# Dealing the work at the ends of the two attention halves: statistics over heads, a tile table moved back, a causal mask by TensorE for two batches

## The reference

```python
x = x + _L0_attn_a_ref(_layernorm(x), wq, bq, wk, bk, wv, bv, wo, bo)    # causal, 16 heads of 8
x = x + _L0_ffn_ref(_layernorm(x), Wr, Wg, Wu, Wd)
x = x + _L0_attn_b_ref(_layernorm(x), W_qkv, b_qkv, W_proj, b_proj)      # not causal, softmax of a
x = x + _L0_ffn_ref(_layernorm(x), Wr, Wg, Wu, Wd)                       # scaled negative distance
```

## Time and profile before

| | us |
|---|---|
| median of 3 timed runs | 1205.51 |
| lowest and highest of them | 1203.42, 1205.73 |
| the profiled execution, its own time | 1201.22 |
| its span, first to last instruction | 1198.8 |
| busy: TensorE | 1031.9 (86%) |
| busy: VectorE | 763.5 (64%) |
| busy: ScalarE | 672.4 (56%) |
| busy: GpSimd | 538.9 (45%) |

### The profile page before, as it was taken

One profiled execution on the slowest core, in us unless ns is written; L12 is line 12 of the kernel. 1 busy time (PEld: TensorE's weight loads), 2 busy tenths in 40 slices (PEclk: granted clock), 3 DMA queues, 4 the chain that ended last, 5 costly groups with the idle time before them and its releaser, 6 DMA issues.

```text
span 1198.8 us, 28758 instructions
## 1 busy us (share of the span) xinstructions
PE 1031.9 (86%) x9198; PEld 719.2 (60%) x9198; DVE 763.5 (64%) x2364; ACT 672.4 (56%) x1399; POOL 538.9 (45%) x1010
## 2 busy tenths in 40 slices
PE   3998999896789989999798879998977689899990
PEld 1444555452358889999444434443443489899990
DVE  5687777968548333366778888888767573234442
ACT  2465767553524445555377769887836445455550
POOL 2243444333850630344688645655626416103555
PEclk9999999996858999999778889998967799999995
DMA  6355444662125877887644324333121258778974
GB/s 158 92 133 142 100 103 98 179 140 61 40 70 154 267 230 235 258 270 221 143 110 100 97 56 108 82 92 84 44 56 58 91 171 282 217 227 263 280 218 111
DMA packets 201722, 175.02 MB, mean 146 GB/s; under 512 B 19812, under 2 KB 160616, under 8 KB 201576
## 3 DMA queue, kind: packets, MB, share of 16 engines
q1 hardware_dynamic: 193384, 156.41, 47.4%
q0 software_dynamic: 8192, 16.79, 4.7%
HBM read 122.99 MB, written 50.14 MB: 144 GB/s over the span
## 4 chain that ended last, share of the span: by engine, by line
PE 44%; DVE 15%; POOL 9%; issue 6%; DMA 4%; SPq 1%; ACT 1%; POOLq 0%; ACTq 0%; DVEq 0%
PE psS L1358 9%; PE psT L1365 9%; PE psO L316 4%; PE psN L1381 4%; PE psO L1381 4%; PE psS L350 3%; POOL xn L1259 3%; DVE mx L662 3%; POOL prow L736 2%; PE psO L959 2%; PE psN L323 1%; PE psT L358 1%; PE psM L1346 1%; DMA eo<-ysb 1%; POOL part L749 1%
## 5 line engine op out<-in xcount | busy, mean ns | idle before, releaser
L662 DVE TENSOR_REDUCE mx<-psS 128x3 f32<-128x384 f32 (+1 forms) x512 | 311.1, 617 | 117.9 <-PE psS L377 62.4
L350 PE MATMUL psS<-kst,qst 48*128 48x256 bf16 (+1 forms) x1024 | 200.9, 284 | 57.2 <-DVE mx L662 42.6
L549 ACT ACTIVATE pT<-psT,scb 128x512 f32<-128x512 f32 x256 | 194.0, 778 | 56.7 <-PE psT L358 55.3
L1421 DVE TENSOR_TENSOR hT<-sg,psT 128x512 f32<-128x512 f32 x142 | 97.5, 686 | 160.3 <-PE psT L1365 126.1
L358 PE MATMUL psT<-qst,kst 50*128 50x256 bf16 (+1 forms) x1024 | 194.0, 279 | 5.4 <-DMA qst<-scr_m 2.4
L1245 POOL DMA_INDIRECT xg<-xn,slot x128 | 123.5, 965 | 149.9 <-DVE ysb L1416 86.5
L780 POOL TENSOR_SCALAR_AFFINE_SELECT pT<-pT 128x256 f32<-128x256 f32 x256 | 104.0, 414 | 134.0 <-ACT pT L544 132.2
L350 PEld LDWEIGHTS psS<-kst,qst 48*128 48x128 bf16 x1024 | 65.7, 97 | 156.8 <-DVE mx L662 82.7
L1358 PE MATMUL psS<-xTt,wgc 128*128 128x128 f32 x1136 | 153.5, 279 | 5.0 <-issue 5.0
L544 ACT ACTIVATE pT<-psT 128x384 f32<-128x384 f32 x256 | 122.6, 491 | 57.7 <-PE psT L358 56.2
L1365 PE MATMUL psT<-xTt,wuc 128*128 128x128 f32 x1136 | 151.8, 277 | 0.4 <-DMA wuc<-in_L_ffn_Wu 0.3
(11 more groups left out here) (227 smaller groups left out, 1605.2 us busy)
## 6 DMA issues: line engine op xcount, KB each, us to landing
wgc<-in_L_ffn_Wg SPq DMA_DIRECT2D x142, 256.0 KB
wuc<-in_L_ffn_Wu SPq DMA_DIRECT2D x142, 256.0 KB
scr_part<-part SPq DMA_DIRECT2D x128, 128.0 KB, 2.1
qst<-scr_part SPq DMA_DIRECT2D x64, 192.0 KB, 3.7
kst<-scr_part SPq DMA_DIRECT2D x64, 192.0 KB, 4.5
xin<-xg SPq DMA_DIRECT2D x142, 64.0 KB
eo<-ysb SPq DMA_DIRECT2D x142, 64.0 KB
scr_part<-part SPq DMA_DIRECT2D x32, 192.0 KB, 1.9
```

Source lines behind the costliest of these rows:

```text
L350: return nc.tensor.matmul(ps[:, c0:c0 + n], q_[r64, t, q0], k_[r64, t, 0:n], start=(half == 0), stop=True, skip_group_check=True)
L549: nc.scalar.activation(pT[:, g % 8, 0:cols], psT[g % 2][:, 0:cols], ACT.Exp, scale=scb[r][:, 0, i:i + 1], bias=scb[r][:, 1, i:i + 1]).then ...
L662: nc.vector.tensor_reduce(mx3[:, u, 0:n, pos:pos + 1].rearrange("p a b -> p (a b)"), psS[h % 2][:, 0:kcols(L)].rearrange("p (a k) -> p a k ...
L1421: nc.vector.tensor_tensor(out=hT[(n0 + k) % FETCH][:].rearrange("p a c -> p (a c)"), in0=sg[p][:], in1=psT[p][:], op=ALU.mult).then_inc(f[ ...
```

## The change

- Steps 17 and 18 of layer 0 (T of the batches 14 and 15, `MASKED = B - 2`): the select on GpSimd and its semaphore go; TensorE adds the mask to T by a matmul of the identity with a second triangle `tritb` over the two diagonal squares; `pv_quad` waits for the exponential. GpSimd makes `tritb` at the start (two operations more).
- Step 18, both layers: the statistics of group 1's 12 blocks are dealt over heads 0 to 8 by `dve_ln_at`, its tokens over heads 10 to 13, three a head.
- Group 0's stage 8 (tile table) goes from step 16, head 5 (layer 0) and step 17, head 2 (layer 1) to step 18, head 15; so does stage 2 (weights) from step 15, head 15 and step 16, head 12.
- Layer 1: the 16 tokens of GpSimd stand as 8 behind the split of step 14 and 8 behind that of step 15.
- Both layers: the load of Silu's activation table stands behind the first two tile copies of the feed-forward part, no more before them.

```diff
@@ pv_quad
-                after(pe, s["pT"], 16 * b + 4 * q + 4)
+                if L.causal and b >= MASKED:
+                    after(pe, s["exp"], 16 * b + 4 * q + 4)
+                else:
+                    after(pe, s["pT"], 16 * b + 4 * q + 4)
@@ pe_step, behind scores_t(1)
+                    if L.causal and bT >= MASKED:
+                        diag = psT[1 - par][:, 0:3 * P].rearrange("p (a k) -> p a k", a=3)[:, 0:3:2, :]
+                        last_t = nc.tensor.matmul(diag, identb[:], tritb[:].unsqueeze(1).to_broadcast([P, 2, P]),
+                                                  start=False, stop=True, skip_group_check=True)
                     last_t.then_inc(s["ST"], 1)
@@ pool_step
                     after(pool, s["exp"], 16 * bT + h + 1)
-                    d = pT[:, (h ^ 1) % 8, 0:384].rearrange("p (a k) -> p a k", a=3)[:, 0:3:2, :]
...
+                    if bT < MASKED:
+                        d = pT[:, (h ^ 1) % 8, 0:384].rearrange("p (a k) -> p a k", a=3)[:, 0:3:2, :]
...
@@ act_tile
             if k == 0:
                 tokens(0)
                 tokens(1)
+                nc.scalar.activation(junk[0:1, 0, 0:1], ones_row[0:1, 0:1], ACT.Silu)
@@ pool_beside
-                if l == 1 and j == 15 and h == 1:
+                if l == 1 and j in (14, 15) and h == H:
                     pool.wait_ge(s_ln[2], 1)
-                    for k in range(SIZE[0]):
+                    for k in range((j - 14) * SIZE[0] // 2, (j - 13) * SIZE[0] // 2):
@@ act_beside
-                if j == 19 and h == 15:
-                    nc.scalar.activation(junk[0:1, 0, 0:1], ones_row[0:1, 0:1], ACT.Silu)
@@ dve_beside
                         dve_counts(dve, 0)
-                        dve_route_part(dve, 0, 2)
-                if l == 0 and j == 16 and h < 6:
+                if l == 0 and j == 16 and h < 5:
                     dve_route_part(dve, 0, h + 3)
...
-                if l == 1 and j == 16 and h == 12:
-                    dve_route_part(dve, n, 2)
...
-                if l == 1 and j == 17 and h < 3:
+                if l == 1 and j == 17 and h < 2:
                     dve_route_part(dve, n, h + 6)
-                if j == 18 and h in (6, 8):
-                    if h == 6:
+                if j == 18 and h == 15:
+                    dve_route_part(dve, n, 8)
+                    dve_route_part(dve, n, 2)
+                if j == 18:
+                    if h == 0:
                         dve.wait_ge(x1, NBLK - 4)
-                        dve_ln_stats(dve, SIZE[0], NBLK - 4, s_ln[n + 1])
-                        dve.wait_ge(s_ln[n + 1], 1)
-                    else:
-                        dve_tokens(dve, n + 1, SIZE[0], NBLK - 4)
+                    dve_ln_at(dve, h, SIZE[0], NBLK - 4 - SIZE[0], s_ln[n + 1], 1)
+                    if 10 <= h < 14:
+                        dve_tokens(dve, n + 1, SIZE[0] + 3 * (h - 10), SIZE[0] + 3 * (h - 9))
```

More of the change, by code:

```diff
@@ L40 @@
 PCH = 23
+MASKED = B - 2
 POS = [8 * (h // 8) + 4 * (h % 2) + (h % 8) // 2 for h in range(H)]
@@ L98, in build @@
         trib = sb("trib", [P, P], BF16)
+        tritb = sb("tritb", [P, P], BF16)
         ones_row = sb("ones_row", [1, T])
@@ L358, in scores_t @@
                     return nc.tensor.matmul(ps[:, c0:c0 + T - q0], k_[m64, t, half * P:half * P + P], q_[m64, t, q0:T],
-                                            start=True, stop=True, skip_group_check=True)
+                                            start=(half == 0 or not L.causal), stop=True, skip_group_check=True)
                 if S_:
@@ L778, in pool_step @@
                     after(pool, s["exp"], 16 * bT + h + 1)
-                    d = pT[:, (h ^ 1) % 8, 0:384].rearrange("p (a k) -> p a k", a=3)[:, 0:3:2, :]
-                    nc.gpsimd.affine_select(out=d, in_=d, compare_op=ALU.is_ge, fill=0.0, base=0,
-                                            pattern=[[0, 2], [1, P]], channel_multiplier=-1).then_inc(s["pT"], 1)
+                    if bT < MASKED:
+                        d = pT[:, (h ^ 1) % 8, 0:384].rearrange("p (a k) -> p a k", a=3)[:, 0:3:2, :]
+                        nc.gpsimd.affine_select(out=d, in_=d, compare_op=ALU.is_ge, fill=0.0, base=0,
+                                                pattern=[[0, 2], [1, P]], channel_multiplier=-1).then_inc(s["pT"], 1)
                     if L.pool_hook:
@@ L1755, in _ @@
             nc.gpsimd.memset(trib[:], 0.0).then_inc(s_const, 1)
-            pool.wait_ge(s_const, 2)
+            nc.gpsimd.memset(tritb[:], 0.0).then_inc(s_const, 1)
+            pool.wait_ge(s_const, 3)
             nc.gpsimd.affine_select(out=ident[:], in_=ident[:], compare_op=ALU.not_equal, fill=1.0, base=0,
@@ L1760, in _ @@
                                     pattern=[[-1, P]], channel_multiplier=1).then_inc(s_const, 1)
+            nc.gpsimd.affine_select(out=tritb[:], in_=tritb[:], compare_op=ALU.is_ge, fill=NEG, base=0,
+                                    pattern=[[1, P]], channel_multiplier=-1).then_inc(s_const, 1)
             for r in range(RING):
@@ L1790, in _ @@
             dve.wait_ge(s_lnA, 1)
-            dve.wait_ge(s_const, 4)
+            dve.wait_ge(s_const, 6)
             nc.vector.tensor_copy(identb[:], ident[:]).then_inc(s_const_dve, 1)
@@ L1805, in _ @@
         def _(pe):
-            pe.wait_ge(s_const, 4)
+            pe.wait_ge(s_const, 6)
             pe_setup(pe, LA)
```

## The result

Four timed runs of the changed kernel have a median of 1173.3 us (1170.0 to 1180.1), four of the kernel before beside them 1205.6 us. The ratio is 0.9731, 95% interval 0.9674 to 0.9788: 2.7% faster. The forecast was 1178.2 us with a range of 1169 to 1193. The profiled execution took 1169.96 us with a span of 1167.8 us, against 1201.2 and 1198.8 before, so 31.0 us of span went where 27.3 had been forecast.

A forecast was written before the change was run, and what follows sets the result against it. The attention ends were taken to be bound by waits and the clock falling after them. Gains of 14.9 us (layer 0) and 12.4 us (layer 1) sum to 27.3 us: 1173.9 us profiled, 1178.2 us by median, range 1169 to 1193.

The forecast's parts named there:

- What bounds the ends: Ends of both attention halves: bound by waits and the clock that falls after them, not by TensorE's work.
- Layer 0, steps 15 and 16: Weights leaving step 15 gain 1.0 us; the tile table leaving step 16 gains TensorE's idle 1.9 us.
- Layer 0, step 17: Select waits 2.8 us and clock 2.6 us gained, 16 added matmuls cost 3.4 us: net gain 2.0 us.
- Layer 0, step 18: Step falls from 22.3 to 14.3 us at the full clock, gain 8.0 us; gain 0 if the clock stays low.
- A: Added matmuls or VectorE waits keep TensorE at 1.2 GHz in layer 0's steps 17 to 19: 1192 us; chance 0.20 with its half.
- Layer 0, step 19 and the start: Faster step 19 at the high clock and Silu's table load hidden: 2.0 us together, between 0.4 and 3.4.
- Layer 1, steps 14 to 16: Splitting GpSimd's row scalings removes VectorE's seed wait and speeds the logits, 6.6 us; weights leaving step 16, 1.0 us.
- Layer 1, behind the slots: Only 4.0 us gained before the scatters bound, plus 0.8 us for the Silu table and early statistics.
- B: Layer 1: second 8 scalings end after VectorE's seed asks, or logits run at the low clock: 1181.5 us; chance 0.10.
- C: VectorE's step 18 tokens lock GpSimd out, lengthening layer 1's scatter chain by some 3.2 us: 1181 us; chance 0.03.
- D: TensorE's wait for layer 1's tile 0 leaves the clock low far into feed-forward, slower than before; 1226 us at 20 tiles; chance 0.03.
- E: Layer 0 gains 19 us, with matmuls at half the row's price and step 19 at full clock: 1173 us; chance 0.12.

The follow-up runs named there:

- tables_back: Changed kernel with group 0's tile table and weights put back where they stood before; 1176.3 us, ratio 0.9746 to the kernel before.
- mask_thrice_2: Changed kernel with each of the 32 added mask matmuls followed by two more that add zeros; 1177.9 us, ratio 0.9791 to the kernel before.
- tokens_back: Changed kernel with GpSimd's 16 row scalings of layer 1 in one block in step 15 again; 1178.7 us, ratio 0.9770 to the kernel before.
- five_less: Changed kernel without the last five of layer 1's 32 scatters (part of the tokens missing); 1172.3 us, ratio 0.9707 to the kernel before.
- lump_back: Changed kernel with group 1's statistics and tokens as two lumps in step 18 again; 1180.7 us, ratio 0.9774 to the kernel before.

## Why the prediction held, and where it missed

**What bounds the ends.** Right: waits, and the clock behind them, not TensorE's work. With the waits for selects gone and the statistics dealt, TensorE ran steps 17 and 18 at the high level. The sum came as near as it did partly by luck: the touched rows of the table miss by -1.2, +2.6, +1.1, +0.6, -0.5 and -1.3 us, 7.3 us without their signs and 1.3 with them.

**Layer 0, steps 15 and 16.** Forecast 2.9 us, measured 1.7 from profile to profile and some 3 over all kernels with either order. Held there; that 1.1 to 1.7 us of it are lost again before feed-forward 0 (tables_back) was not in the prediction.

**Layer 0, step 17.** Forecast 2.0, measured 4.6 us. The mis-sized term is the price of the added matmul. I took 0.21 us, the distance from the existing mask matmul to the next score matmul, because the shape is the same. But that distance belongs to the step from the mask to what stands behind it, here the pairs of the scores, and it is paid once a head, however many masks stand before it (mask_thrice_2: 0.20 us behind the last of four). Nor is it the price of standing behind a pair, as the prediction reads the row: from the pair of T to the mask it is 0.15 us, with the change and without. In step 17 the added one stands in front of another full-row matmul and costs 0.12 us, 1.9 us a step instead of 3.4. The estimate of 0.11 us by the Trainium skill ("TensorE: Matmul & The Clock Gate", section "Back-to-back issue gap"), which the prediction set aside, is what the trace after and mask_thrice_2 show for this neighbourhood (0.12 us, and 0.10 to 0.12 us). That is 1.5 of the 2.6 us missed. The other 1.1 are in the waits and the clock, taken at 5.4 us; by the trace they were 4.6 + 1.9 = 6.5.

**Layer 0, step 18.** Forecast 14.3 us for the step, measured 13.2. The matmul price explains 1.1 (3.4 us forecast, an estimate of 2.3 from the trace, above); the second transposes waited almost not at all where 1.5 us had been set down; without both it would have been 11.7 us, so that the work itself was estimated 1.5 us too low. The gain of 8.0 was given to the step as a whole; the runs show that it is one only together: 4.8 us of it stand behind the lump, and without the mask the dealt statistics, with the table behind them, bring 0.5 us. The prediction's 22 us for the step at the low clock do not follow from its own terms: twice 9.4 and 5.1 are 23.9, a loss of 1.6 us and not 0, by which A would have given 1194 us, outside the range.

**Layer 0, step 19 and the start.** Forecast 2.0, measured 2.6, with the clock at 0.75 instead of 0.50. The end is now bound by the scatters as well: a wait of 0.6 us for the first tile. The prediction had the scatters ready 5 us before step 19 needs them, and said nothing of this wait. The step that failed there is the count: at the start of step 17 there were 26 scatters left and not 23, and three waits for exponentials added 2.1 us, so the last ended at 337.4 us, 6.9 us into step 19. The Silu table was not tried apart.

**Layer 1, steps 14 to 16.** Forecast 6.6 + 1.0, measured 7.1; tokens_back gives 6.6 for the split alone, half of it the wait and half the logits at the high clock. The weights' 1.0 is nearer to 0.3 by tables_back.

**Layer 1, behind the slots.** Forecast 4.0 + 0.8, measured 3.5. The mechanism is the one forecast: five_less gives back 5.0 us, and lump_back and tables_back exchange their wait for that of the first tile. From the first scatter to the first tile copy the prediction had 43.4 us (904.82 to 948.2), and it took 43.7. The 0.8 us for the Silu table and the early statistics were wrong in kind, since nothing ahead of a tile that comes late can bring anything.

**The rivals.** Nothing of A is left: the added matmuls don't lower the clock, not even three times as many. B didn't come: the seed did not wait, and the logits ran at 3.74 us. C had asked for 3.2 us more in layer 1's chain of scatters; from the first start to the last the 32 take 39.43 us where they took 39.30. Two of them last 1.00 and 1.04 us instead of 0.96, and that is all that the trace shows of it. D's trigger came, 5.40 us of idle TensorE, but the clock was at 0.97 from 4 us later on, and feed-forward 1 became no longer. E was the likeliest in hindsight: half the matmul's price and a faster step 19, with 18.6 us in layer 0 where it has 19 (its own terms sum to 19.7), and 1173 us. It had a chance of 0.12, since the row was read as evidence against it.

## What to carry to other kernels

Price an added matmul by what stands behind it, and not only by its shape: the distance to the next instruction belongs to the pair (0.12 us here in step 17, up to 0.22 in step 18). Two causes of one stall can be worth more together than one at a time (here 9.6 and 0.5 us apart, 16.2 together), so before giving up an edit that brings nothing, ask what waits next to it. And where a queue of DMAs already bounds the end, time gained on another engine turns into idle time there, unless it also starts the queue sooner.

## What the runs showed of the hardware

- A mask matmul of 256 bf16 columns over all 128 rows costs 0.11 to 0.12 us in front of another such matmul. From such a one to the next pair of scores (48 or 50 rows) it is 0.20 to 0.22 us, to products with V (128 rows, 32 columns) 0.20 to 0.21, to a transpose 0.11 to 0.12 (changed kernel and mask_thrice_2, 2.4 GHz).
- 32 indirect DMAs of 128 rows from GpSimd follow one another every 1.26 us (878.28 to 917.71 us), 0.96 of it the instruction. A faster TensorE and VectorE's tokens beside them changed that by 0.1 us over the whole chain, in two scatters of 1.00 and 1.04 us.
- After 5.4 us of idle time TensorE was granted 0.50 of its clock (1.2 GHz) in the next 4 us and 0.97 in the 10 us after that (changed kernel, 921.95 to 936.00 us).
- The kernel before took 3% longer in one session than in the others (1245 against 1206 us), and step 17 of layer 0, with the order of the changed kernel, 19.6 us instead of 15.5 at a granted clock of 1.00 both times, with instructions of the same length and more idle time between them.
